# Projecting 63 of a graph's 64 nodes on the right side of a two-layer graph attention kernel

## The chip, the core and the metric

The kernel runs on one core of a Trainium2 chip. The metric is the device time of one execution in microseconds (us), the lower the better. The engines are TensorE (PE, with its weight loads listed apart as PEld), VectorE (DVE), ScalarE (ACT), GpSimd (POOL) and SyncE (SP), which issues most DMAs.

## What is computed

There are 128 graphs of 64 nodes with 768 features each. After a layer norm and a ReLU, two layers of the following run, and the input is added at the end:

```python
adj_tri = jnp.triu(adj, k=1)
diag_mask = jnp.triu(adj, k=0) - adj_tri
h = hidden_state
for l in range(L):
    m_left = jnp.einsum('bsh,oh->bso', h, W_left[l])
    m_right = jnp.einsum('bsh,oh->bso', h, W_right[l])
    u_left = jnp.einsum('bih,bjh->bij', h, m_left) / temper
    u_right = jnp.einsum('bih,bjh->bij', h, m_right) / temper
    u = u_left * adj_tri + u_left * diag_mask + u_right * jnp.swapaxes(adj_tri, 1, 2)
    delta_exp_u = jnp.exp(u) * adj
    attention = delta_exp_u / (jnp.sum(delta_exp_u, axis=2, keepdims=True) + 1e-10)
    h_lin = jnp.einsum('bsh,oh->bso', h, W_lin[l]) + b_lin[l]
    ctx = jnp.matmul(attention, h_lin)
    h = jax.nn.relu(_layer_norm(ctx, ln_a[l], ln_b[l]))
```

In the sum for `u` the right scores are multiplied by the transposed strict triangle: entry (i, j) counts only where i > j. For i = 0 there is no such j, so the right scores of row i = 0 are always multiplied by zero.

## The kernel before

**Tiles and groups.** A tile is 128 rows of `h`, that is two graphs. A group is four tiles (`TILES`), eight graphs. Each layer has 16 groups, so there are 32 groups in all. Every product is made in three passes over operands that are split into a high and a low part of type float32r (`PASSES`, line 47): high by high, low by high, high by low.

**The buffer of the split rows.** `ht` (line 190) holds the transposed rows of a group, with the features on the partitions. Within a tile, a part's 128 columns are ordered by node and then by graph: column 2n + b is node n of graph b (`ht_half`, line 278, and `by_graph`). So the first two columns of a tile are node 0 of both graphs.

**The projections (M steps).** `project` (line 541) does one job k of 12: the block `oc = k // 2` of 128 output features, and the side `k % 2` (0 left, 1 right). The left and right weights are taken untransposed, so the job projects each node i to the vector that is later multiplied by the rows of all j. A job has 6 feature blocks by 3 passes, that is 18 matmuls over all four tiles, with 512 columns each, into one of two banks of `pm` (`M_BANKS`). The jobs k = 0 and k = 1 are done in two halves of two tiles each (`m_parts`, line 57), so they take 36 matmuls of 256 columns each. A right-side matmul thus has 512 columns for k = 3, 5, 7, 9, 11 and 256 columns for k = 1.

**Emptying a job.** ACT writes the high part of the bank into `gt` (line 678), and DVE writes the low part (line 754, through the helper at line 722). Both read through `by_node`, which turns the order by node into an order by graph, and write through `gt_part`. TensorE may start job k when the job k - 2 has been emptied (`m_clear`, line 573).

**The scores (S steps).** Line 597 multiplies a tile's `ht` columns by 256 columns of `gt`: for one graph, its 64 columns of both parts and both sides. There are 8 such matmuls for each block `oc`, and 6 blocks in a group.

**After the scores.** U, EX, EM, EP and ET make the masked exponentials. H (line 609) makes the third projection in jobs of 18 matmuls with 384 columns each. C (line 633) multiplies both. T (line 537) transposes the rows of the next group with 128-column matmuls. F normalises. A (line 620) transposes adjacency tiles with 128-column matmuls in layer 0. `mask` has the triangles in it already: line 795 multiplies the scores by them.

**What sets the order.** The order of the steps is written out by hand in `iteration_steps` (line 99) and `m_phase_steps` (line 64), and every engine walks the same list. Each engine is its own queue and waits on semaphores. The middle groups are loops whose bodies are one group.

**Start.** POOL sets the constants (lines 483 to 506) and counts `const_ready` up to 10; PE, ACT and DVE wait for that before their first work. SP issues the first loads of rows, weights, adjacency and vectors without waiting for POOL (lines 405 to 411). The next load of rows (line 399, called at line 426) waits for the transposes of tile 0 (line 424).

The functions touched by the change are `gt_part` (line 286), `by_node` (line 290), the POOL block (line 482), the PE block (line 527) with `project`, and the places at lines 678 and 753 that call `by_node`.

Of the kernel before, what the change touches and what calls it, by code (L numbers as in the profile page):

```python
# [36 lines left out]
F32 = mybir.dt.float32  # L37
# [5 lines left out]
HI, LO = 0, 1  # L43
LEFT, RIGHT, LIN = 0, 1, 2
ML, ADJ, MR = 0, 1, 2

PASSES = ((HI, HI), (LO, HI), (HI, LO))

M_BANKS = 2
C_BANKS = 2  # L50
TILES = 4
# [101 lines left out]
def gnn_kernel(nc, x, adj, w_left, w_right, w_lin, b_lin, ln_a, ln_b, h1, adj_t, out):  # L153
    B, S, _ = adj.shape
    H = x.shape[2]
    L = w_left.shape[0]
    P = 128
# [23 lines left out]
    with ExitStack() as ctx:  # L181
# [3 lines left out]
        def sem(name):  # L185
            return ctx.enter_context(nc.semaphore(name))


        wt = sb("wt", [P, 3, 2, KC, H], F32R)
        ht = sb("ht", [P, KC, TILES, 2, P], F32R)  # L190
        gt = sb("gt", [P, 2, 2, 2, ROWS], F32R)
# [30 lines left out]

        const_base = sem("const_base")
        const_ready = sem("const_ready")
        vec_loaded = sem("vec_loaded")
        adj_loaded = sem("adj_loaded")
        adj_t_stored = sem("adj_t_stored")
# [5 lines left out]
        m_hi = sem("m_hi")  # L233
# [48 lines left out]
        def by_graph(tiles):  # L282

            return tiles.rearrange("p c (b n) -> p c b n", b=2)

        def gt_part(k, part):

            return gt[:, k // 2 % 2, part, k % 2, :].rearrange("p (t b n) -> p t b n", t=TILES, b=2)

        def by_node(bank):  # L290

            return bank.rearrange("p (t n b) -> p t b n", t=TILES, b=2)


# [186 lines left out]
        @block.gpsimd  # L481
        def _(pool):
            nc.gpsimd.memset(ident[:], 0.0).then_inc(const_base, 1)
            nc.gpsimd.memset(until[:], 1.0).then_inc(const_base, 1)
            nc.gpsimd.memset(beyond[:], 1.0).then_inc(const_base, 1)
            nc.gpsimd.memset(ebd[:], 0.0).then_inc(const_ready, 1)
            nc.gpsimd.memset(powers[:, 0:1], 0.5).then_inc(const_ready, 1)
            nc.gpsimd.memset(powers[:, 1:2], -0.5).then_inc(const_ready, 1)
            nc.gpsimd.memset(unit[:, HI, :], 1.0).then_inc(const_ready, 1)
            nc.gpsimd.memset(unit[:, LO, :], 0.0).then_inc(const_ready, 1)  # L490
            pool.wait_ge(const_base, 3)
            pool.wait_ge(const_ready, 5)

            nc.gpsimd.affine_select(out=ident[:], in_=ident[:], compare_op=ALU.not_equal, fill=1.0, base=0,
                                    pattern=[[1, P]], channel_multiplier=-1).then_inc(const_ready, 1)

            for b in range(2):

                own = slice(b * S, (b + 1) * S)
                pool.wait_ge(const_ready, 6 + 2 * b)  # L500
                nc.gpsimd.affine_select(out=until[own, :], in_=until[own, :], compare_op=ALU.is_ge, fill=0.0, base=0,
                                        pattern=[[-1, S]], channel_multiplier=1).then_inc(const_ready, 1)
                pool.wait_ge(const_ready, 7 + 2 * b)
                nc.gpsimd.affine_select(out=beyond[own, :], in_=beyond[own, :], compare_op=ALU.is_gt, fill=0.0, base=0,
                                        pattern=[[1, S]], channel_multiplier=-1).then_inc(const_ready, 1)
            pool.wait_ge(const_ready, 10)

            def walk(part, G):
                first, end, looped, steps, _, _ = part
                for step in steps:  # L510
                    kind = step[0]
                    if kind == "C":
                        t = step[1]
                        pool.wait_ge(c_var, tile_count(G, t + 1))
                        nc.gpsimd.tensor_tensor(col[:, STD, t:t + 1], col[:, VAR, t:t + 1], powers[:, 0:1],  # L515
                                                ALU.pow).then_inc(c_std, 1)
                    if kind == "X":
                        t = step[1]
                        pool.wait_ge(x_var, tile_count(G + step[2], t + 1))
                        nc.gpsimd.tensor_tensor(col[:, XRSTD, t:t + 1], col[:, XVAR, t:t + 1], powers[:, 1:2],  # L520
                                                ALU.pow).then_inc(x_rstd, 1)

            each_part(pool, walk)
# [2 lines left out]
        @block.tensor  # L526
        def _(pe):
            pe.wait_ge(const_ready, 10)

            def transposes(part, G, step, source):  # L530

# [9 lines left out]
            def project(k, t0, t1, c0, c1):  # L541

                oc, lr = k // 2, k % 2
                for kc in range(c0, c1):
                    for n, (a, b) in enumerate(PASSES):
                        last = nc.tensor.matmul(pm[:, k % M_BANKS, t0 * P:t1 * P], wt[:, lr, a, kc, oc * P:(oc + 1) * P],  # L546
                                                ht[:, kc, t0:t1, b, :], start=(kc == 0 and n == 0),
                                                stop=(kc == KC - 1 and n == len(PASSES) - 1))
                return last

# [93 lines left out]
        def _(act):  # L644
# [5 lines left out]
            def walk(part, G):  # L650
# [3 lines left out]
                for step in steps:  # L654
# [14 lines left out]
                    elif kind == "V":  # L669
                        _, slot, count = w_slot(first, step)  # L670
                        act.wait_ge(w_loaded[slot], count)
                        _, mat, ob = step
                        nc.scalar.copy(wt[:, mat, HI, :, ob * P:(ob + 1) * P],
                                       side[:, slot, :].rearrange("p (c n) -> p c n", c=KC)).then_inc(v_hi, 1)
                    elif kind == "M" and step[3] == TILES and step[5] == KC:
                        k = step[1]
                        act.wait_ge(m_full, M_JOBS * N + k + 1)
                        nc.scalar.copy(gt_part(k, HI), by_node(pm[:, k % M_BANKS, :])).then_inc(m_hi, 1)  # L678
                    elif kind == "H":
                        t, half = step[1:]  # L680
                        j = H_JOB + 2 * t + half
                        act.wait_ge(m_full, M_JOBS * G + j + 1)
                        nc.scalar.copy(hl[:, H_SLOTS[t], HI, SUMS + half * HALF:SUMS + (half + 1) * HALF],  # L683
                                       pm[:, j % M_BANKS, 0:HALF]).then_inc(m_hi, 1)
                    elif kind == "U":

                        p = step[1]
                        wait_from(act, stored[p], 32 * G)
                        act.wait_ge(u_full, tile_count(G, 2 * p + 2))
                        for b in range(2):  # L690
                            near, far = slice(b * S, (b + 1) * S), slice((1 - b) * S, (2 - b) * S)
                            nc.scalar.copy(parted[p][near].rearrange("p t a m j -> p t (a m j)"),
                                           pu[far, 2 * p:2 * p + 2, b * 2 * P:(b + 1) * 2 * P]).then_inc(u_cross, 1)
                    elif kind == "EX":
                        act.wait_ge(u_summed, pair_count(G, 2))
                        nc.scalar.activation(us[:], us[:], ACT.Exp, scale=INV_TEMPER).then_inc(e_exp, 1)
                    elif kind == "ET":
                        act.wait_ge(e_moved, 32 * G + 32)
                        nc.scalar.copy(et[:, :, HI, :], ebd[:]).then_inc(et_hi, 1)
                    elif kind == "N":  # L700
                        t = step[1]
                        act.wait_ge(x_shift, tile_count(G + step[2], t + 1))
                        row = rows[:, H_SLOTS[t], :]
                        nc.scalar.activation(row, row, ACT.Relu, bias=col[:, XSHIFT, t:t + 1],  # L704
                                             scale=col[:, XRSTD, t:t + 1]).then_inc(x_norm, 1)
                    elif kind == "F" and layer == 0:
                        t = step[1]
                        act.wait_ge(f_affine, tile_count(G, t + 1))
                        nc.scalar.activation(side[:, t % 2, :], side[:, t % 2, :], ACT.Relu).then_inc(f_done, 1)  # L709
# [5 lines left out]
        def _(dve):  # L715
# [5 lines left out]
            def low_part(dst, src, hi):  # L721
                return nc.vector.tensor_tensor(dst, src, hi.bitcast(F32), ALU.subtract)  # L722

            def walk(part, G):
# [3 lines left out]
                for step in steps:  # L728
# [21 lines left out]
                    elif kind == "M" and step[3] == TILES and step[5] == KC:  # L750
                        k = step[1]
                        dve.wait_ge(m_hi, M_JOBS * N + k + 1)
                        low_part(gt_part(k, LO), by_node(pm[:, k % M_BANKS, :]), gt_part(k, HI)).then_inc(m_clear, 1)
                    elif kind == "H":
                        t, half = step[1:]
                        j = H_JOB + 2 * t + half
# [154 lines left out]
```

## Time and profile before

| what | value |
|---|---|
| time, median of 3 runs | 2858.11 us |
| lowest and highest of the 3 | 2855.97 and 2859.23 us |
| the profiled execution, span from first to last instruction | 2857.3 us |
| instructions in the span | 43013 |
| PE busy | 2820.9 us (99%) |
| PEld busy | 2577.6 us (90%) |
| DVE busy | 1546.2 us (54%) |
| ACT busy | 691.1 us (24%) |
| POOL busy | 109.6 us (4%) |

For the profiled execution the trace gives the span alone, and it lies within the three times. Its matmuls overlap each other, so a matmul's mean duration is longer than the spacing from one to the next; the spacing is read from the chain of work that ended last, where a run of matmuls stands with its count and the time that it took.

### The profile page before, as it was taken

Reading aid. Unit: us, or ns where it says so; the run is one execution under the profiler, and the core shown is the slowest. Engines: PE = TensorE matmul, PEld = TensorE weight load, DVE = VectorE, ACT = ScalarE, POOL = GpSimd, SP = SyncE. Lnnn points to the kernel's source line nnn. Section 1 sums busy time; section 2 is a strip of 40 time slices with the busy share of each in tenths; the row PEclk is TensorE's granted clock in tenths of the full one; section 3 lists DMA queues with packets and bytes.
Section 4 is the critical chain, followed back from the end, with each engine's and each line's share of the span. In section 5 each row is a group of like instructions: output and inputs, shape, how many; then the busy total and the mean of one; then the engine's idle time right before and its main releaser. Section 6 shows DMA issues by size and latency. Waiting matters only on the chain.

```text
span 2857.3 us, 43013 instructions
## 1 busy us (share of the span) xinstructions
PE 2820.9 (99%) x15880; PEld 2577.6 (90%) x15880; DVE 1546.2 (54%) x3426; ACT 691.1 (24%) x1271; POOL 109.6 (4%) x209
## 2 busy tenths in 40 slices
PE   7999999999999999999999999999999999999997
PEld 6999899998899988999989999899998899998996
DVE  5555565555555555655555555455545555554556
ACT  3322222322223222232332222112221122221121
POOL 0000000000000000000000000000000000000000
PEclk9999999999999999999999999999999999999998
DMA  5111011110111111111241121121211111111211
GB/s 160 40 41 42 34 51 40 46 44 26 49 40 46 44 40 35 46 46 52 62 127 57 55 61 61 55 72 50 61 61 53 63 54 56 61 61 55 72 34 57
DMA packets 127178, 157.63 MB, mean 55 GB/s; under 512 B 65440, under 2 KB 83872, under 8 KB 127136
## 3 DMA queue, kind: packets, MB, share of 16 engines
q1 hardware_dynamic: 125984, 153.91, 17.6%
q10 hardware_dynamic: 1152, 3.15, 0.4%
q8 instruction: 28, 0.46, 0.1%
q14 instruction: 14, 0.11, 0.0%
HBM read 100.40 MB, written 52.43 MB: 53 GB/s over the span
## 4 chain that ended last, share of the span: by engine, by line
PE 98%; DVE 1%; DMA 1%; SPq 0%; ACT 0%; issue 0%; DVEq 0%; ACTq 0%
PE pm L546 55%; PE pm L609 28%; PE pu L597 6%; PE pc L633 5%; PE pc L537 3%; DMA rows<-in_x_dram 0%; DMA side<-in_L_gnn_W_lin_dram 0%; PE pu L620 0%; SPq L389 0%; SPq L378 0%; DVE side L789 0%; DVE rows L852 0%; DVE side L852 0%; DVE rows L842 0%; DVE side L842 0%
## 5 line engine op out<-in xcount | busy, mean ns | idle before, releaser
L546 PE MATMUL pm<-ht,wt 128*128 128x256 f32 (+1 forms) x8064 | 1636.5, 360 | 1.3 <-DVE ht L722 1.3
L546 PEld LDWEIGHTS pm<-ht,wt 128*128 128x128 f32 x8064 | 1352.7, 189 | 215.6 <-issue 1.7
L609 PE MATMUL pm<-wt,ht 128*128 128x384 f32 x4608 | 845.4, 337 | 0.6 <-DVE hl L722 0.6
L609 PEld LDWEIGHTS pm<-wt,ht 128*128 128x128 f32 x4608 | 794.0, 188 | 6.8 <-DVE hl L722 6.8
L722 DVE TENSOR_TENSOR gt<-pm,gt 128x512 fp32r<-128x512 f32 x384 | 265.4, 691 | 814.4 <-ACT gt L678 814.4
L678 ACT CAST gt<-pm 128x512 fp32r<-128x512 f32 x384 | 224.0, 583 | 1197.6 <-PE pm L546 1197.6
L722 DVE TENSOR_TENSOR hl<-pm,hl 128x384 fp32r<-128x384 f32 x256 | 142.5, 557 | 390.6 <-ACT hl L683 389.6
L683 ACT CAST hl<-pm 128x384 fp32r<-128x384 f32 x256 | 123.0, 480 | 551.1 <-PE pm L609 551.1
L597 PEld LDWEIGHTS pu<-gt,ht 128*128 128x128 f32 x1536 | 211.6, 196 | 9.7
L597 PE MATMUL pu<-gt,ht 128*128 128x256 f32 x1536 | 214.7, 282 | 0.0
L633 PE MATMUL pc<-hl,et 128*128 128x386 f32 (+1 forms) x768 | 158.7, 342 | 3.1 <-DVE et L722 1.8
L515 POOL TENSOR_TENSOR col<-col,powers 128x1 f32<-128x1 f32 x128 | 72.1, 563 | 2087.4 <-DVE col L836 2087.4
L633 PEld LDWEIGHTS pc<-hl,et 128*128 128x128 f32 x768 | 137.9, 190 | 9.1 <-DVE et L722 2.3
L822 DVE SCALAR_TENSOR_TENSOR side<-vec,col,pc 128x384 f32<-128x384 f32 x252 | 143.7, 612 | 4.5
L722 DVE TENSOR_TENSOR ht<-pc,ht 128x384 fp32r<-128x384 f32 x256 | 130.2, 550 | 2.8 <-ACT ht L661 2.6
L852 DVE SCALAR_TENSOR_TENSOR side<-side,col,vec 128x768 f32<-128x768 f32 x126 | 128.3, 1019 | 4.4
L828 DVE BATCH_NORM_STATS2 stats<-side 128x6 f32<-128x384 f32 x252 | 127.8, 550 | 0.0
L842 DVE SCALAR_TENSOR_TENSOR side<-side,mom,vec 128x768 f32<-128x768 f32 x126 | 127.3, 1010 | 0.5
L537 PE MATMUL pc<-ident,rows 128*128 128x128 f32 x768 | 106.4, 275 | 14.5 <-ACT rows L704 11.6
L661 ACT CAST ht<-pc 128x384 fp32r<-128x384 f32 x256 | 116.4, 516 | 5.2 <-PE pc L537 4.9
L709 ACT ACTIVATE side<-side 128x768 f32<-128x768 f32 x64 | 54.2, 846 | 253.4 <-DVE side L852 253.4
L537 PEld LDWEIGHTS pc<-ident,rows 128*128 128x128 f32 x768 | 92.2, 141 | 19.5 <-issue 10.7
(60 smaller groups left out, 848.5 us busy)
## 6 DMA issues: line engine op xcount, KB each, us to landing
rows<-in_x_dram SPq DMA_DIRECT2D x64, 384.0 KB, 3.2
h_dram<-side SPq DMA_DIRECT2D x64, 384.0 KB, 2.3
rows<-h_dram SPq DMA_DIRECT2D x64, 384.0 KB, 3.2
side<-in_x_dram SPq DMA_DIRECT2D x64, 384.0 KB, 3.3
out_dram<-side SPq DMA_DIRECT2D x62, 384.0 KB, 2.6
mask<-in_adj_dram SPq DMA_DIRECT2D x48, 128.0 KB, 3.6
side<-in_L_gnn_W_left_dram SPq DMA_DIRECT2D x12, 384.0 KB, 3.7
side<-in_L_gnn_W_right_dram SPq DMA_DIRECT2D x12, 384.0 KB, 3.6
```

The lines of the kernel that those rows point to most:

```text
L537: last = nc.tensor.transpose(pc[:, half, j * P:(j + 1) * P], source[:, kc * P:(kc + 1) * P], ident[:])
L546: last = nc.tensor.matmul(pm[:, k % M_BANKS, t0 * P:t1 * P], wt[:, lr, a, kc, oc * P:(oc + 1) * P], ht[:, kc, t0:t1, b, :], start=(kc == 0 ...
L597: last = nc.tensor.matmul(pu[:, t, b * 2 * P:(b + 1) * 2 * P], h_parts[:, b, :], gt[:, oc % 2, :, :, own], start=(oc == 0 and b == 0), sto ...
L609: last = nc.tensor.matmul(pm[:, j % M_BANKS, 0:HALF], ht[:, kc, t, a, :], wt[:, LIN, b, kc, half * HALF:(half + 1) * HALF], start=(n == 0) ...
L633: last = nc.tensor.matmul(pc[:, half, 0:own.stop - own.start], et[:, t, a, :], hl[:, H_SLOTS[t], b, own], start=(n == 0), stop=(n == 2))
L678: nc.scalar.copy(gt_part(k, HI), by_node(pm[:, k % M_BANKS, :])).then_inc(m_hi, 1)
L683: nc.scalar.copy(hl[:, H_SLOTS[t], HI, SUMS + half * HALF:SUMS + (half + 1) * HALF], pm[:, j % M_BANKS, 0:HALF]).then_inc(m_hi, 1)
L722: return nc.vector.tensor_tensor(dst, src, hi.bitcast(F32), ALU.subtract)
L822: nc.vector.scalar_tensor_tensor(out=context[:, at], in0=vec[:, 0, at], scalar=col[:, ESUM, t:t + 1], in1=pc[:, half, behind:behind + HALF ...
L828: nc.vector.bn_stats(stats[:, half, :], context[:, half * HALF:(half + 1) * HALF]).then_inc(c_stats, 1)
L842: nc.vector.scalar_tensor_tensor(out=row, in0=row, scalar=mom[:, t, 0:1], in1=vec[:, 1, :], op0=ALU.subtract, op1=ALU.mult).then_inc(f_cen ...
L852: nc.vector.scalar_tensor_tensor(out=row, in0=row, scalar=col[:, SCALE, t:t + 1], in1=vec[:, 2, :], op0=ALU.mult, op1=ALU.add).then_inc(f_ ...
```

## The change

The right side of a job has 126 columns for a tile in place of 128: the two columns of node 0 are left out. The bank then holds 4 x 126 columns (or 2 x 126 in a half job). ACT and DVE read the shorter bank and write nodes 1 to 63 into `gt`. The columns of node 0 of the right side in `gt` are set to zero once at the start, by four memsets on POOL, and stay so. PE has one more wait at its start, for these memsets.

```diff
+RIGHT_SIDE = 1
...
+        first_zero = sem("first_zero")
...
+        def nodes(k):
+
+            return S - k % 2
+
         def gt_part(k, part):
 
-            return gt[:, k // 2 % 2, part, k % 2, :].rearrange("p (t b n) -> p t b n", t=TILES, b=2)
-
-        def by_node(bank):
-
+            both = gt[:, k // 2 % 2, part, k % 2, :].rearrange("p (t b n) -> p t b n", t=TILES, b=2)
+            return both[:, :, :, k % 2:S]
+
+        def by_node(k):
+
+            bank = pm[:, k % M_BANKS, 0:TILES * 2 * nodes(k)]
             return bank.rearrange("p (t n b) -> p t b n", t=TILES, b=2)
...
             nc.gpsimd.memset(beyond[:], 1.0).then_inc(const_base, 1)
+            for half in range(2):
+                for part in (HI, LO):
+                    unused = gt[:, half, part, RIGHT_SIDE, :].rearrange("p (g n) -> p g n", n=S)[:, :, 0:1]
+                    nc.gpsimd.memset(unused.bitcast(F32), 0.0).then_inc(first_zero, 1)
             nc.gpsimd.memset(ebd[:], 0.0).then_inc(const_ready, 1)
...
             pe.wait_ge(const_ready, 10)
+            pe.wait_ge(first_zero, 4)
...
                 oc, lr = k // 2, k % 2
+                cols = 2 * nodes(k)
                 for kc in range(c0, c1):
                     for n, (a, b) in enumerate(PASSES):
-                        last = nc.tensor.matmul(pm[:, k % M_BANKS, t0 * P:t1 * P], wt[:, lr, a, kc, oc * P:(oc + 1) * P],
-                                                ht[:, kc, t0:t1, b, :], start=(kc == 0 and n == 0),
+                        last = nc.tensor.matmul(pm[:, k % M_BANKS, t0 * cols:t1 * cols], wt[:, lr, a, kc, oc * P:(oc + 1) * P],
+                                                ht[:, kc, t0:t1, b, P - cols:P], start=(kc == 0 and n == 0),
                                                 stop=(kc == KC - 1 and n == len(PASSES) - 1))
...
-                        nc.scalar.copy(gt_part(k, HI), by_node(pm[:, k % M_BANKS, :])).then_inc(m_hi, 1)
+                        nc.scalar.copy(gt_part(k, HI), by_node(k)).then_inc(m_hi, 1)
...
-                        low_part(gt_part(k, LO), by_node(pm[:, k % M_BANKS, :]), gt_part(k, HI)).then_inc(m_clear, 1)
+                        low_part(gt_part(k, LO), by_node(k), gt_part(k, HI)).then_inc(m_clear, 1)
```

## Rows read from the trace of the kernel before

**Rows 1.** The page: span, busy engines, TensorE's clock in 40 slices, the chain.

```profile
span 2857.3 us, 43013 instructions
...
PE 2820.9 (99%) x15880; PEld 2577.6 (90%) x15880; DVE 1546.2 (54%) x3426; ACT 691.1 (24%) x1271; POOL 109.6 (4%) x209
...
PEclk9999999999999999999999999999999999999998
...
PE 98%; DVE 1%; DMA 1%; SPq 0%; ACT 0%; issue 0%; DVEq 0%; ACTq 0%
```

**Rows 2.** Waits of PE: line, waited for: us in total, times, longest.

```profile
PE pc L537 <- ACT rows L704: 11.6, 2, 7.5
...
PE pc L633 <- DVE et L722: 1.8, 1, 1.8
PE pm L546 <- DVE ht L722: 1.3, 1, 1.3
```

**Rows 3.** Groups of PE's instructions, shapes apart: count | busy us, mean ns | idle before.

```profile
L546 PE MATMUL pm<-ht,wt 128*128 128x512 f32 x5760 | 1347.7, 391 | 0.0
L609 PE MATMUL pm<-wt,ht 128*128 128x384 f32 x4608 | 845.4, 337 | 0.6 <-DVE hl L722 0.6
L546 PE MATMUL pm<-ht,wt 128*128 128x256 f32 x2304 | 291.4, 285 | 1.3 <-DVE ht L722 1.3
L597 PE MATMUL pu<-gt,ht 128*128 128x256 f32 x1536 | 214.7, 282 | 0.0
...
L537 PE MATMUL pc<-ident,rows 128*128 128x128 f32 x768 | 106.4, 275 | 14.5 <-ACT rows L704 11.6 <-DVE ht L722 2.9
```

**Rows 4.** The chain in order of time, 1070 to 1130 us: start us, us, what, count.

```profile
1070.83 3.12 PE pm L609 x18
1073.95 0.66 PE pc L537 x6
...
1078.41 6.46 PE pm L546 x54
...
1088.08 0.44 PE pu L620 x4
...
1097.80 0.95 PE pu L597 x8
...
1107.89 4.10 PE pm L546 x18
...
1118.12 8.19 PE pm L546 x36
```

**Rows 5.** Groups of the instructions that write `gt`, on DVE and ACT.

```profile
L722 DVE TENSOR_TENSOR gt<-pm,gt 128x512 fp32r<-128x512 f32 x384 | 265.4, 691 | 814.4 <-ACT gt L678 814.4
...
L678 ACT CAST gt<-pm 128x512 fp32r<-128x512 f32 x384 | 224.0, 583 | 1197.6 <-PE pm L546 1197.6
```

**Rows 6.** Timeline, 0 to 20 us: start us, us, engine, line, operation [idle before, releaser].

```profile
1.12 0.52 POOL L486 MEMSET ebd<- 128x512 f32 x1
1.58 0.10 POOL L487 MEMSET powers<- 128x1 f32 x1
1.61 0.10 POOL L488 MEMSET powers<- 128x1 f32 x1
...
3.35 0.24 POOL L504 TENSOR_SCALAR_AFFINE_SELECT beyond<-beyond 64x64 bf16<-64x64 bf16 x1
...
3.94 1.02 DVE L865 BATCH_NORM_STATS2 xstats<-rows 128x6 f32<-128x384 f32 x2 [2.96 <-DMA rows<-in_x_dram]
...
7.46 1.51 PE L537 MATMUL pc<-ident,rows 128*128 128x128 f32 x6 [7.46 <-ACT rows L704]
```

**Rows 7.** The chain in order of time, 0 to 45 us, at the fourth load of rows.

```profile
11.16 0.43 SPq L389
11.60 0.04 issue
11.64 9.06 DMA rows<-in_x_dram
```

## The prediction, made before the changed kernel ran

> **What bounds the kernel now.** I read the page first. PE is busy for 99% of the span, the chain of work that ended last is 98% PE, and TensorE's clock is granted in full, 2.4 GHz, in nearly every slice [rows 1]. So the time is the time of the matmuls, and an edit is worth what it takes out of PE's stream. Then I read what PE waits for: its longest wait is 7.5 us and belongs to the start; the projections at L546 waited once, for 1.3 us [rows 2]. No other engine holds PE up once the groups run. Third come the groups of PE's instructions with the shapes kept apart: the 512-column and the 256-column matmuls of L546 are the ones that the change cuts [rows 3]. Their mean durations overlap, so they are no prices. The price is the spacing, which I read from the chain in order of time: a run of one kind with its count and its time [rows 4].
>
> **The price of a column.** All from [rows 4]. Eighteen matmuls of 512 columns took 4.10 us, 227.8 ns each. Fifty-four of 256 columns took 6.46 us, 119.6 ns each. The slope is (227.8 - 119.6) / 256 = 0.423 ns a column, and what is left at no columns is 119.6 - 256 x 0.423 = 11.4 ns. The line is tested by a third width: at 384 columns it gives 173.7 ns, and eighteen such matmuls took 3.12 us, 173.3 ns each. So between 256 and 512 columns a matmul of these operands costs 11.4 ns and 0.423 ns for each column, and nothing else shows. One more reading matters for the new operand, which is 126 columns of each tile in turn: L597 reads its 256 columns in four pieces of 64, and eight of them took 0.95 us, 118.8 ns each, no more than L546's two pieces of 128. Pieces cost nothing by that.
>
> The Trainium skill has a rule that speaks against this price: the page "TensorE: Matmul & The Clock Gate", section "Back-to-back issue gap", gives a sustained spacing of about 81 ns at 128 columns and 131 ns at 512 for a stream of weight loads and matmuls. That slope is 0.13 ns a column, and by it the sum below would be, as an estimate, 3.6 us in place of 11.7. The trace does not agree: at 512 columns it shows 227.8 ns, not 131 [rows 4], so I give the rule no chance of its own.
>
> **The change, part by part.**
>
> *The right-side jobs k = 3, 5, 7, 9, 11.* Of the 5760 matmuls of 512 columns [rows 3], five jobs in ten are right ones: 2880. Each goes to 504 columns, inside the tested widths: 8 x 0.423 = 3.38 ns. In all 2880 x 3.38 = 9.7 us. It all lies on the path, since PE is the path.
>
> *The right-side job k = 1.* Of the 2304 matmuls of 256 columns [rows 3], half are right ones: 1152. They go to 252 columns, which is narrower than any matmul of split operands in the trace. On the line this saves 4 x 0.423 = 1.69 ns each, 1.9 us in all. The trace has no such width, so I bound it. The lower bound is the line. The nearest narrower rows are the 128-column transposes: four took 0.44 us and six took 0.66 us, 110 ns each [rows 4], where the line would give 65.5. They are above the line, at 0.859 ns a column. At that rate 252 columns would take 216.5 ns, 96.9 ns more than now, and 1152 of them 111.6 us. The two ends are 1.9 us saved and 111.6 us lost. I take the line: 252 is 4 columns from a point on it and 124 from the transposes, which are another operation, on plain float32 operands.
>
> *The emptying by ACT and DVE.* Half of the 384 jobs write 504 elements in place of 512, in runs of 63. ACT takes 583 ns and DVE 691 ns for a job now, and both idle ahead of it, ACT for 1197.6 us in all and DVE for 814.4 [rows 5]. A job of 512 columns lasts 4.10 us on PE, and a bank is wanted again only when the other bank's job has ended. The two together take 1.27 us of that; even if the shorter runs doubled both, 2.55 us would fit. I cost it at nothing either way. The cover would be gone only if they took over 4.10 us together.
>
> *The four memsets on POOL.* They stand in POOL's queue ahead of the rest of the constants, so that `const_ready` comes later. Small memsets take 0.10 us each, started 0.03 apart; the largest took 0.52 [rows 6]. So four cost between 0.1 and 2.1 us of POOL's time, nearer to the small ones at 8 elements a partition: up to 0.4 us. POOL ends its constants at 3.59 us, and DVE's first work starts at 3.94, when the first rows land [rows 6]. With 0.4 us more it starts some 0.05 us later. That does not reach the end either: PE's first transposes end at 8.97 us [rows 6], while the load that waits for them is issued at 11.64, straight behind SP's own earlier issues, and this load is what the chain follows up to 20.70 us [rows 7]. There are 2.6 us to spare, more than the upper bound of 2.1. I cost the memsets at nothing.
>
> *The wait of PE for the memsets.* It stands in front of PE's whole queue, but PE's first transposes wait for ACT until 7.46 us [rows 6], long after POOL is through. Nothing.
>
> *What is unchanged.* The number of matmuls, weight loads, DMAs and other waits stays; PE's scores at L597 still read 256 columns, the zeros among them.
>
> *What is late next.* PE comes 0.36 us sooner through each of the 32 groups (11.7 / 32). DVE at 54% and ACT at 24% [rows 1] have to follow in 0.36 us less for each group and have the room, so no new wait is due.
>
> **The sum.** 9.7 + 1.9 = 11.7 us with the rounding left to the end (9.74 + 1.95). Against the profiled span that is 2857.3 - 11.7 = 2845.6 us. The trace gives no other time for that execution; its span lies 0.8 us under the median of the three runs, 2858.1, and within their spread. I predict the median: 2858.1 - 11.7 = 2846.4 us, 0.4% less. About 0.2% (5.7 us) is what a measurement of this kernel can tell from no change, so the forecast is faster by twice that.
>
> **The rivals.**
>
> *The narrow matmuls leave the line (slower).* One mechanism, at the two halves of job k = 1: TensorE takes matmuls that are narrower than 256 columns at another rate. For it: no matmul of split operands under 256 columns is in the trace, and the only narrower ones, the transposes, cost 110 ns where the line gives 65.5 [rows 4]. Against it: these transposes differ in operation and type, so their rate may belong to that and not to the width; and the line shows no bend down to 256. The price at their rate is 111.6 us less the 9.7 of the wide jobs: 2858.1 + 111.6 - 9.7 = 2960 us. It decides from 8.5 ns extra for a narrow matmul (9.74 us / 1152), where it eats the whole gain. I give it 0.20.
>
> The Trainium skill, page "FP8 and Floating Point Precision", section "TensorE Precision Notes", says that true float32 takes four passes through the array and that a reduced-precision float32 exists beside it; it does not say when the one turns into the other. If the narrow matmuls fell to four passes, the estimate would be 1008 columns on the line, 437.5 ns, and 3214 us in all; no run so far shows it.
>
> *Width buys nothing (no change).* The moving operand is fetched in whole aligned pieces, so that 126 columns which start 8 bytes into a tile cost as much as 128 from its start, at both widths. For it: the widths that price the line, 256, 384 and 512, are all multiples of 128, and these matmuls start at a tile's first column. Against it: the line through the three is smooth [rows 4], though such a grain would not show in it. The time is then 2858 us. That the slices in the diff did not shorten the matmuls at all would give the same; the shapes in the diff speak against that. Together 0.16.
>
> The Trainium skill names such pieces: the page "SBUF — State Buffer", in the section on the DMA port swizzle, speaks of 16-byte lines and a penalty for each line crossed. By it 126 columns from byte 8 touch 32 lines, as many as 128 columns do, which is this rival's no gain; no run here shows the lines.
>
> **How the numbers follow.** The forecast, faster along the line, has 0.64; no change 0.16; slower 0.20. The likeliest case's own range is 2844 to 2850 us: at the low end the full 11.7 us from a run near the lowest of the three (2855.97), at the high end only the wide jobs gain (2858.1 - 9.7 = 2848.4) with the spread of the three runs above it. The range that holds 8 in 10 reaches to the no-change case with its spread, 2843.5 to 2859.5, and leaves the slower rival out. The cases give faster 0.64, within 0.2% 0.16, slower 0.20.
>
> **What would show each step right or wrong.** In the profile after, the groups by shape should show 2880 matmuls of L546 with 504 columns and 1152 with 252. In the chain, eighteen of 504 columns should take 4.04 us (224.4 ns each) where eighteen of 512 still take 4.10, and eighteen of 252 should take 2.12 us (117.9 ns) beside 2.15 for 256. A run of eighteen narrow ones at 3.9 us would be the slower rival; 4.10 us at 504 columns would be the no-change one. The waits of PE should stay the handful at the start; a new one on `m_clear`, from DVE at L722, would prove the emptying mis-costed, and a later end of the fourth load of rows than 20.70 us would prove the memsets mis-costed.

## The result and the profile after

The changed kernel takes 2874.14 us (median of 5 runs, 2873.72 to 2874.35) against 2856.57 us before in the same comparison: a ratio of 1.006, 95% interval 1.0049 to 1.007. It is slower by 17.6 us, where 11.7 us less were predicted.

The page after shows the same picture as [rows 1], with the added time on TensorE alone:

```profile
span 2872.5 us, 43018 instructions
...
PE 2835.7 (99%) x15880; PEld 2575.7 (90%) x15880; DVE 1543.7 (54%) x3426; ACT 690.0 (24%) x1271; POOL 109.7 (4%) x213
...
PEclk9999999999999999999999999999999999999998
...
PE 98%; DVE 1%; DMA 1%; SPq 1%; ACT 0%; issue 0%; DVEq 0%; ACTq 0%
```

The clock did not change and PE is still the bound. (A time lies some 1.8 us above its span: this profiled execution took 2874.26 us. So the profiled execution before, with a span of 2857.3 us, was one of the slowest of its kernel, and the spans differ by 15.2 us only.) The waits of PE after answer to [rows 2]:

```profile
PE pc L550 <- ACT rows L718: 10.5, 2, 7.5
PE pc L550 <- DVE ht L736: 4.0, 1, 4.0
...
PE pm L560 <- DVE ht L736: 1.6, 2, 1.3
```

No new wait holds PE up. The groups after, which answer to [rows 3], show the new shapes:

```profile
L560 PE MATMUL pm<-ht,wt 128*128 128x504 f32 x2880 | 700.0, 396 | 0.0
L560 PE MATMUL pm<-ht,wt 128*128 128x512 f32 x2880 | 685.5, 391 | 0.0
...
L560 PE MATMUL pm<-ht,wt 128*128 128x256 f32 x1152 | 152.6, 287 | 1.6 <-DVE ht L736 1.6
L560 PE MATMUL pm<-ht,wt 128*128 128x252 f32 x1152 | 147.2, 281 | 0.0
```

The change does what it says: 2880 matmuls have 504 columns and 1152 have 252. But a matmul of 504 columns lasts 396 ns, longer than one of 512 with 391. The narrow ones seem to get shorter. The chain of the changed kernel in order of time (start, us, what, count) gives the spacing, as in [rows 4]:

```profile
1084.37 6.46 PE pm L560 x54
...
1091.89 2.11 PE pm L560 x18
...
1094.43 8.34 PE pm L560 x36
...
1104.79 8.32 PE pm L560 x36
...
1114.07 4.09 PE pm L560 x18
...
1119.23 4.14 PE pm L560 x18
...
1124.33 8.33 PE pm L560 x36
...
1133.62 8.32 PE pm L560 x36
```

The chain of the kernel before has the same pieces, beside those of [rows 4]:

```profile
1085.93 2.15 PE pm L546 x18
...
1088.51 8.21 PE pm L546 x36
...
1098.76 8.18 PE pm L546 x36
...
1113.06 4.11 PE pm L546 x18
```

The piece of 18 ahead of the first 36 is the second half of k = 1 at 252 columns: 2.11 us, where the kernel before took 2.15. The first half lies within the piece of 54, which takes 6.46 us as before [rows 4]: there the four columns were worth nothing. A piece of 36 is a left job and a right job in turn (k = 2 and 3, then 4 and 5): 8.34 and 8.32 us against 8.21 and 8.18. The left job k = 6 alone still takes 4.09 us, so a right job takes about 4.23 us, 235 ns a matmul in place of 227.8, where 4.04 us were due.

For a finer reading, I take the start times of the trace's records and the gaps from one matmul of a job to the next: the mean of the sixth to the seventeenth gap, over all groups, without gaps above 300 ns, in which another step stands between. A spacing below is this mean. Left jobs: 226.7 to 227.7 ns before and 226.7 to 226.9 after. Right jobs k = 3, 5, 9, 11: 226.7 ns before, 234.5 after; k = 7, which follows other work: 230.1. Summed over the four pieces of the chain the right jobs lose 0.57 us a group (0.13 to 0.14 us each, and 0.03 for k = 7, whose eighteen take 4.14 us, against 4.11 in the chain before), times 32 groups 18 us, less 1.3 us (0.04 x 32) for the second half of the narrow job: about 17 us, which is the loss.

### The profile page after: what moved, and what is told of

Its sections match the earlier page's. It is cut to its first block, busy times and chain, and to the rows that moved or that the text cites. A ratio compares the mean times of both kernels' runs of the same rounds, so it can differ in the third digit from the quotient of the medians.

```text
span 2872.5 us, 43018 instructions
## 1 busy us (share of the span) xinstructions
PE 2835.7 (99%) x15880; PEld 2575.7 (90%) x15880; DVE 1543.7 (54%) x3426; ACT 690.0 (24%) x1271; POOL 109.7 (4%) x213
## 3 DMA queue, kind: packets, MB, share of 16 engines
q1 hardware_dynamic: 125984, 153.91, 17.6%
q10 hardware_dynamic: 1152, 3.15, 0.4%
## 4 chain that ended last, share of the span: by engine, by line
PE 98%; DVE 1%; DMA 1%; SPq 1%; ACT 0%; issue 0%; DVEq 0%; ACTq 0%
PE pm L560 55%; PE pm L623 28%; PE pu L611 6%; PE pc L647 5%; PE pc L550 3%; DMA rows<-in_x_dram 0%; DMA side<-in_L_gnn_W_lin_dram 0%; PE pu L634 0%; SPq L397 0%; SPq L386 0%; DVE side L803 0%; SPq L407 0%; DVE rows L866 0%; DVE side L866 0%; DVE rows L856 0%
## 5 line engine op out<-in xcount | busy, mean ns | idle before, releaser
L560 PE MATMUL pm<-ht,wt 128*128 128x256 f32 (+3 forms) x8064 | 1651.5, 362 | 1.6 <-DVE ht L736 1.6
L736 DVE TENSOR_TENSOR gt<-pm,gt 128x512 fp32r<-128x512 f32 (+1 forms) x384 | 263.4, 686 | 830.3 <-ACT gt L692 830.3
L692 ACT CAST gt<-pm 128x512 fp32r<-128x512 f32 (+1 forms) x384 | 222.8, 580 | 1212.8 <-PE pm L560 1212.8
```

The source lines that it names most:

```text
L560: last = nc.tensor.matmul(pm[:, k % M_BANKS, t0 * cols:t1 * cols], wt[:, lr, a, kc, oc * P:(oc + 1) * P], ht[:, kc, t0:t1, b, P - cols:P], ...
L692: nc.scalar.copy(gt_part(k, HI), by_node(k)).then_inc(m_hi, 1)
```

## The experiments

**The wide jobs alone.** k = 1 goes back to 256 columns:

```diff
-            return S - k % 2
+            return S - (1 if k % 2 and k > 1 else 0)
...
-            return both[:, :, :, k % 2:S]
+            return both[:, :, :, S - nodes(k):S]
```

> Only the right-side jobs k = 3, 5, 7, 9, 11 are narrowed to 504 columns; k = 1 keeps its 256 columns. In the changed kernel the 504-column matmuls follow each other at about 234 ns, not the 224 of the line, where the 512-column ones still take 228. All theories agree here: if the loss is in the wide jobs alone (6 ns x 2880 = 17 us), this kernel takes about 2874 to 2875 us, since k = 1 gains about 1 us at 252 columns. If the narrow job had a part in the loss, it would take under 2870 us.

2875.97 us, ratio to before 1.0074 (1.0057 to 1.0091). The loss is the wide jobs'.

**The narrow job alone.** Only k = 1 is cut (`1 if k == 1 else 0`).

> The change at the job k = 1 alone: 1152 matmuls of 252 columns, and all wide jobs at 512. By the prediction's line it gains 1.9 us; by the chain of the changed kernel (eighteen in 2.11 us against 2.15) about 1.3 us; by the slower rival of the prediction it loses. About 2855 us, not to be told from no change.

2855.14 us, ratio 0.9995 (0.9985 to 1.0004): no change that can be measured, as expected. The matmuls of 252 columns take some 120 ns in the first half of k = 1 and 117 in the second, against 120 at 256 columns in the kernel before and 117.9 on the line. The slower rival of the prediction is out.

**Start, run or width.** Three kernels change the moving operand of the wide right-side jobs. The first takes the first 126 columns of a tile:

```diff
...
-                                                ht[:, kc, t0:t1, b, P - cols:P], start=(kc == 0 and n == 0),
+                                                ht[:, kc, t0:t1, b, 0:cols], start=(kc == 0 and n == 0),
```

> As the kernel with the wide jobs alone, but the 126 columns of a tile are its first ones (nodes 0 to 62), so that the moving operand starts where the tile starts; the right scores of node 63 are left out of those blocks. Theory A, the start 8 bytes into a tile is what costs: the spacing falls to the line's 224.4 ns and the time to 2858 - 9.7 = about 2847 us. Theory B, runs of 126 columns with jumps between them are what costs, and theory C, the width of 504 itself breaks the rhythm of weight loads and matmuls: the spacing stays at 234 ns and the time at 2874 us.

The second keeps 512 columns and moves the start (`first` is 2 for the high part and 126 for the low part, in the tile's 256 columns of both):

```diff
...
+                return ht[:, kc, t0:t1].rearrange("p t a n -> p t (a n)")[:, :, first:first + P]
...
```

> The kernel before with its 512 columns and runs of 128, but in the right-side jobs from k = 3 on each run starts off the tile's start, 8 bytes past a 16-byte boundary, so it reads two columns of the neighbouring part (the right scores of those blocks are of other data). Theory A (the start): the spacing rises from 228 to about 238 ns, the time to about 2858 + 28 = 2886 us. Theories B (runs of 126) and C (the width of 504): the spacing stays at 228 ns and the time at 2858 us.

The third reads 504 columns in one unbroken run:

```diff
...
+                return ht[:, kc].rearrange("p t a n -> p (t a n)")[:, b * 512:b * 512 + 504]
...
```

> As the kernel with the wide jobs alone, but the 504 columns are one unbroken run that starts at the buffer's first column of the feature block (for the low part, at column 512), so the right scores of those blocks are of other data. Theory A (the start) and theory B (the short runs with jumps): the spacing falls to 224.4 ns and the time to about 2847 us. Theory C (the width of 504 as such): the spacing stays at 234 ns and the time at 2874 us.

| kernel | time, us | ratio to before | spacing in right jobs, ns |
|---|---|---|---|
| 504 from the first column | 2856.32 | 1.0002 (0.9992 to 1.0012) | 226.7 |
| 512, shifted start | 2901.20 | 1.0162 (1.0145 to 1.0179) | 242.2 |
| 504 in one run | 2857.06 | 1.0003 (0.9993 to 1.0012) | 226.7 |

The chain of the kernel with 504 from the first column shows a pair of jobs (k = 4 and 5) in the time of before:

```profile
1098.94 8.19 PE pm L560 x36
```

The chain of the kernel with the shifted start shows the same pair:

```profile
1112.89 8.46 PE pm L553 x36
```

No theory had it all. The start costs: 15.5 ns at full width, and the whole loss goes when the 504 columns start with the tile. Runs do not count here: one run or four give 226.7 ns. But from an aligned start 504 columns cost exactly what 512 cost, so the line of the prediction fails there too.

**A ladder of widths.** Each of the five right jobs gets another width, from an aligned start, once as one run and once as four:

```diff
-            return S - (1 if k % 2 and k > 1 else 0)
+            return {3: 62, 5: 61, 7: 60, 9: 59, 11: 56}.get(k, S)
...
```

The single runs are read as in the kernel with one run, the four as in the one with the first columns.

> The five wide right-side jobs read one unbroken run from an aligned start, each of another width: 496, 488, 480, 472 and 448 columns for k = 3, 5, 7, 9, 11 (the right scores of those blocks are of other data and partly left out). Theory D, TensorE's time goes in blocks of 16 columns (504 costs what 512 costs): 220.0, 220.0, 213.3, 213.3 and 200.0 ns, 38 us less than before in all, about 2818 us. Theory E, blocks of 32 columns: 226.7, 226.7, 213.3, 213.3 and 200.0 ns, about 2825 us. The line of the prediction: 220.9, 217.5, 214.2, 210.8 and 200.6 ns, about 2814 us.

> As the run before it, with the same five widths, but as four runs of a quarter each that start at the tiles' first columns (124, 122, 120, 118 and 112 columns a run; the last nodes' right scores are left out). If only the width of the whole matmul is rounded up, the five spacings are those of the single runs. If each run is rounded up by itself, to 16 columns, they are 226.7, 226.7, 226.7, 226.7 and 200.0 ns; to 4 columns (16 bytes), 220, 223, 213, 213 and 200 before the whole is rounded.

| columns | the prediction's line, ns | one run, ns | four runs, ns |
|---|---|---|---|
| 504 | 224.6 | 226.7 | 226.7 |
| 496 | 221.2 | 220.0 | 225.0 |
| 488 | 217.8 | 224.2 | 224.5 |
| 480 | 214.4 | 216.7 | 216.7 |
| 472 | 211.1 | 213.6 | 213.4 |
| 448 | 200.9 | 202.7 | 204.8 |

One run each: 2825.14 and 2829.26 us, against 2859.93 for the kernel before beside them. Neither blocks of 16 nor of 32 columns fit: 488 takes longer than 496, in one unbroken run. And runs do count at some widths: at 496 columns four cost 5 ns more than one. The line is off by 1 to 7 ns at these widths, and what a cut of 8 columns is worth on it, 3.4 ns, lies within that error.

**A ladder of starts.** All jobs at 512 columns, the starts of the right ones 2, 4, 8, 16 and 32 columns off:

```diff
...
+                off = {3: 2, 5: 4, 7: 8, 9: 16, 11: 32}[k]
+                first = P - off if b == LO else off
...
```

> The full 512 columns in four runs of 128 in all jobs, but in the right-side jobs k = 3, 5, 7, 9, 11 each run starts 2, 4, 8, 16 and 32 columns (8, 16, 32, 64 and 128 bytes) off the tile's start (the right scores of those blocks are of other data). An eighteen at a shift of 2 took 4.36 us before (242 ns), against 4.10 (227.8). If the grain of the start is 16 bytes, only the job k = 3 is slow and the time is about 2865 us; 32 bytes: k = 3 and 5, about 2874 us; 64 bytes: k = 3, 5 and 7, about 2883 us; if any start off the tile's is slow, all five, about 2901 us.

Spacing 242.2, 229.0, 233.1, 230.9 and 233.3 ns; 2878.32 us in one run of the kernel. The chain of that kernel has the five in order (k = 2 and 3; 4 and 5; 6; 7; 8 and 9; 10 and 11):

```profile
1097.34 8.49 PE pm L568 x36
...
1107.87 8.23 PE pm L568 x36
...
1117.05 4.10 PE pm L568 x18
...
1122.22 4.19 PE pm L568 x18
...
1127.37 8.28 PE pm L568 x36
...
1136.61 8.30 PE pm L568 x36
```

The start of 8 bytes is the worst, but even 128 bytes (k = 11) cost 6.6 ns. So no grain of up to 128 bytes in the start alone explains it.

**Starts and cuts together.** Five operands in one kernel:

```diff
...
+                whole = ht[:, kc].rearrange("p t a n -> p (t a n)")
+                if k == 3:
+                    return whole[:, b * 512 + 2:b * 512 + 2 + 4 * cols]
+                off = {5: 4, 7: 8, 9: 2, 11: 16}[k]
+                return ht[:, kc, t0:t1, b, off:off + cols]
...
```

> Starts and cuts together, in the right-side jobs: k = 3 one unbroken run of 504 columns from column 2; k = 5 four runs of 124 from column 4; k = 7 four of 120 from column 8; k = 9 four of 124 from column 2 (ending short of the tile's end); k = 11 four of 112 from column 16. If the start costs something for each run, k = 3 is near 228 to 229 ns (a quarter of the 7 ns that four runs cost at 504); if it costs by the matmul, 234 ns. If only starts off a 16-byte boundary cost, k = 5, 7 and 11 have the spacing of their widths from an aligned start, and k = 9 lies some 7 ns above its own.

Spacing 230.0 ns (504 in one run from column 2), 226.2 (four of 124 from column 4), 220.0 (four of 120 from column 8), 233.3 (four of 124 from column 2) and 204.8 (four of 112 from column 16); 2844.93 us in one run of the kernel. At 124 columns a run, column 2 costs 8.3 ns over the aligned 225.0, and column 4 costs 1.2; column 8 costs 3.3 at 120 columns, and column 16 nothing at 112. One run from column 2 costs 3.3 ns, four cost 7.8: more than a quarter, so the price is neither by the run nor by the matmul alone.

**The rows' buffer or the weights moved.** In the changed kernel, `ht` goes 56 bytes on, or `wt` 8 bytes on:

```diff
-        ht = sb("ht", [P, KC, TILES, 2, P], F32R)
+        ht = sb("ht", [P, KC * TILES * 2 * P + 16], F32R)[:, 14:14 + KC * TILES * 2 * P].rearrange(
+            "p (c t a n) -> p c t a n", c=KC, t=TILES, a=2)
```

The move of the weights is written in the same way, with `2:` in place of `14:`. It makes `wt` 64 bytes longer, so the buffers behind it, `ht` first, lie 64 bytes further on.

> The changed kernel with the buffer of the split rows put 56 bytes further on, so that column 2 of a tile lies on a 64-byte boundary and column 0 lies 8 bytes ahead of one. Theory A1, the start matters by its own address: the right-side jobs of 504 columns fall from about 234 to 226.7 ns (as from the first column), and the left-side jobs of 512, which now start off the boundary, rise from 226.7 to about 242; in all about 2857 + 45 = 2902 us. Theory A2, what matters is where the moving operand lies against the weights that are read at the same time: the same, since the weights have not moved. Theory A3, the start within the tile matters and not the address: nothing changes, 2874 us.

> The changed kernel with the weights put 8 bytes further on, the split rows on a 64-byte boundary as before, so that the 504 columns from column 2 lie against the weights as 512 columns from column 0 did. Theory A1 (the moving operand's own address): nothing changes in these jobs, about 234 ns and 226.7 ns, 2874 us (the third projection, which reads the weights as its moving operand, may change). Theory A2 (the address against the weights): the right-side jobs fall to 226.7 ns and the left-side ones rise above it.

With the rows moved, right jobs take 230.0 ns and left jobs 241.1 (2911.54 us); with the weights moved, right jobs take 230.0 and left jobs 230.7 (2881.10 us). The chain with the rows moved, at k = 2 and 3:

```profile
1107.10 8.49 PE pm L561 x36
```

The chain with the weights moved, at k = 4 and 5:

```profile
1106.13 8.29 PE pm L561 x36
```

The second kernel is not the one that its expectation describes, since the rows move too: by 64 bytes, with the weights 8 bytes on. In both kernels the rows so lie 56 bytes further from the weights than before. The right jobs take 230.0 ns in both, but the left ones take 241.1 and 230.7: the distance between the two (theory A2) does not settle the price alone. Theory A1 had the left jobs right with the rows moved (about 242 ns), but it foresaw 226.7 ns for the right ones, and nothing new with the weights moved, as the rows lie on a 64-byte boundary there too; it falls as well, and so does A3. That the place of the weights counts cannot be read from this pair; the kernels with shifted weights below show it.

**Both moved by 8 bytes,** in the kernel before, with the two edits above and `2:` in both:

> The kernel before, with 512 columns everywhere, but both the weights and the split rows put 8 bytes further on. The two have the same place against each other as before. If only that place counts, the 512-column matmuls stay at 226.7 ns and the time at 2857 us. If the start of the moving operand counts by its own address, they rise to about 241 ns (as when the split rows alone were off) and the time to about 2857 + 5760 x 14.5 ns + the narrow ones = 2941 us or more.

2961.99 us, 242.2 to 244.4 ns in all wide jobs. The chain has a pair of jobs (k = 2 and 3) at 8.74 us, against 8.21 before:

```profile
1126.53 8.74 PE pm L548 x36
```

Here too the longer `wt` pushes `ht` on, so that the rows move by 72 bytes and the weights by 8, and they lie 64 bytes further apart than the expectation has it. The kernels with shifted weights below have that distance without a start off the boundary, where the weights are read 16 columns ahead: 512 columns take 229.0 ns there. So the distance is not everything: at the same distance, both operands 72 bytes further on, 8 bytes off their 64-byte boundary, cost 13 to 15 ns more.

**One weight for all.** The right jobs load the same weight columns eighteen times:

```diff
...
+                if lr == 1 and k > 1:
+                    a, kc = HI, 0
+                return wt[:, lr, a, kc, oc * P:(oc + 1) * P]
...
```

> The changed kernel, but the right-side jobs from k = 3 on load the same 128 weight columns for all 18 matmuls (wrong right scores), so that the weights' addresses stop changing from matmul to matmul. If the loss comes from the moving operand alone, the spacing stays at 234 ns and the time at 2874 us. If it comes from weight reads that collide with the moving reads by address, the spacing changes, by more than 2 ns in either direction.

2874.73 us and 234.5 ns in k = 3, 5, 9, 11, 230.1 in k = 7, the same to 0.1 ns. This did not settle what it was meant to: the blocks that a job reads lie whole multiples of 1024 bytes apart, so a place that counts within a shorter stretch was left as it was.

**The weights shifted.** The weights are read some columns ahead of their place, under 504 columns from the first column and from column 2:

```diff
...
+                at = oc * P + {1: -2, 2: -4, 3: -8, 4: -16, 5: -64}.get(oc, 0)
+                return wt[:, lr, a, kc, at:at + P]
...
```

The second kernel has the shifts -2, -4, -16, -32 and -64 in the same place. No buffer moves in either.

> The 504 columns from the tile's first column (226.7 ns, as the 512 ones), with the weights read 2, 4, 8, 16 and 64 columns ahead of their place for the jobs k = 2 and 3, 4 and 5, 6 and 7, 8 and 9, 10 and 11 (all scores wrong from there on). If rounding of the width alone keeps 504 from gaining, all five stay at 226.7 ns. If the weight reads get in the way of the moving reads, the spacing at 504 changes with the shift and for some shift falls towards the line's 223 to 224 ns, and the 512-column jobs change too (with the weights 8 bytes off they took 230.7).

> The 504 columns from column 2 (234.5 ns) with the weights read 2, 4, 16, 32 and 64 columns ahead for the five pairs of jobs. If the start of the moving operand alone costs, all five right-side jobs stay at 234 ns. If it is the moving reads against the weight reads, they differ by the shift, 230 ns or less at some; a shift with less than 226 ns at 504 and 226.7 at 512 would allow a kernel that beats both.

| weights ahead by, columns | 504 from column 0, ns | 512 beside it, ns | 504 from column 2, ns | 512 beside it, ns |
|---|---|---|---|---|
| 2 | 233.3 | 233.3 | 231.0 | 233.3 |
| 4 | 226.7 | 226.8 | 231.3 | 228.4 |
| 8 | 226.7 | 233.3 | - | - |
| 16 | 230.0 | 229.0 | 226.7 | 229.0 |
| 32 | - | - | 233.3 | 232.6 |
| 64 | 226.7 | 226.8 | 234.5 | 226.7 |

(2866.67 and 2878.45 us, one run each.) The chain of the first shows its pair at a shift of 2 columns (k = 2 and 3), in 8.38 us against 8.21 before:

```profile
1090.88 8.38 PE pm L566 x36
```

With nothing changed but the address of the weights, the same matmuls go from 226.7 to 233.3 ns and back. No shift brought 504 columns under 226.7. And for the slow start at column 2, a shift of 16 columns gave 226.7 (in k = 7, which the change alone had at 230.1), while for the start at column 0 the same shift cost 3.3 ns. So neither place has a price of its own: with the weights in place column 0 is the fast start, with the weights 16 columns ahead it is column 2.

**The loss taken back.** So the last kernel is the changed kernel whole, with the right side's weights moved on by 448 bytes, and the third projection's weights and all buffers behind them by 512. Counted within blocks of 512 bytes, the right side's weights alone move, 64 bytes nearer to the start:

```diff
-        wt = sb("wt", [P, 3, 2, KC, H], F32R)
+        whole = sb("wt", [P, 3 * 2 * KC * H + P], F32R)
...
+                first = mat * 2 * KC * H + (0, P - 16, P)[mat]
...
```

> The changed kernel with nothing left out, and the right side's weights alone put 16 columns (64 bytes) nearer to the start of a 512-byte block than the others; left side and third projection keep their places. With the weights read 16 columns ahead, one job of 504 columns from column 2 took 226.7 ns. If the loss of the change is where the two reads lie against each other, all right-side jobs fall from 234.5 to about 226.7 ns and the time to about 2874 - 2880 x 7.5 ns = 2853 to 2857 us, level with the kernel before. If the start at column 2 costs by itself, or that one job was a lucky phase, they stay at 230 to 234 ns and the time at 2863 to 2874 us.

2856.94 us, ratio to the kernel before 1.0002 (0.9992 to 1.0011). Its groups show the 504-column matmuls at 390 ns in place of 396:

```profile
L569 PE MATMUL pm<-ht,wt 128*128 128x504 f32 x2880 | 682.5, 390 | 0.0
```

Its chain shows a pair of jobs at 8.19 us, as before the change:

```profile
1098.26 8.19 PE pm L569 x36
```

The spacing is 226.7 to 226.8 ns in all five right jobs. The whole loss is gone, with the same columns from the same start, as expected. The rows moved by 512 bytes as well, which was not tested apart; but the left jobs, whose weights stayed, kept 226.7 to 227.8 ns, and in the changed kernel the jobs k = 3, 5, 9 and 11 took 234.5 ns alike, with weights that start whole multiples of 512 bytes apart.

## Why the prediction was wrong

**Right.** PE bounds the kernel before and after. The memsets cost nothing that the runs show: the four took 0.22 us of POOL and ended the constants at 3.73 us in place of 3.59, and DVE started at 3.84 us, as the rows landed.

The timeline of the changed kernel, from its start, has it:

```profile
1.12 0.22 POOL L497 MEMSET gt<- 128x8 f32 x4
...
3.49 0.24 POOL L516 TENSOR_SCALAR_AFFINE_SELECT beyond<-beyond 64x64 bf16<-64x64 bf16 x1
...
3.84 1.02 DVE L879 BATCH_NORM_STATS2 xstats<-rows 128x6 f32<-128x384 f32 x2 [2.86 <-DMA rows<-in_x_dram]
```

One of the prediction's own signs did come up. The fourth load of rows was issued at 12.72 us in place of 11.64 [rows 7], and landed at 21.17, later than 20.70:

```profile
12.72 8.45 DMA rows<-in_x_dram
```

Without the memsets it was issued at 10.56 and 11.48 in two experiments, and with them at 11.11 to 11.74 in three more and at 12.20 in a fourth. The two overlap, so this is taken for SP's own spread; at 0.5 us it would be a small part of the 17.6 in any case. Emptying stayed hidden: ACT took 577 ns and DVE 682 for the cut jobs, a little less than [rows 5], and runs of 63 cost nothing. That pieces cost nothing held for 504 columns from the tile's start, where one run and four took the same; it did not hold from column 2 (230.0 ns in one run, 234.5 in four) or at 496 columns (220.0 and 225.0). The term of k = 1 had the right sign: 1.3 us by the chain instead of 1.9, all of it in the second half.

**The step that failed** is the first term, "Each goes to 504 columns, inside the tested widths: 8 x 0.423 = 3.38 ns". It was to gain 9.7 us and lost about 18. It failed twice. First, the three widths of the line, 256, 384 and 512, do not test what lies between them, and the one in the middle is of L609, where the weights are streamed and the rows loaded: from an aligned start 504 columns take 226.7 ns, not 224.6 or less, and around them the widths scatter by several ns. That took the gain. Second, the term priced the columns and not the address: it left out that the operand now starts 8 bytes into a tile, against weights that stay where they were. That added 7.8 ns to a matmul (3.4 in k = 7). The prediction did name the new start, in the no-change rival, but bounded it at no gain; it gave no rival in which the start costs more than the columns save. An operand that no row showed was bounded from one side only.

**The rivals.** The slower one had the right sign for a wrong cause: it put the loss on the narrow matmuls, which lost nothing. The no-change one had half of the cause, a fetch that does not get cheaper by eight columns. Its mechanism of whole pieces is not borne out: 488 columns took longer than 496, and the changed kernel's 504 longer than 512. By the rule of 16-byte lines from the Trainium skill, page "SBUF — State Buffer", section on the DMA port swizzle, the cut operand would, as an estimate, cost what the full one costs; the trace shows 234.5 ns against 226.7, so the rule does not give this loss.

**The cause, as far as it is shown.** The loss depends on where the moving operand and the weights lie. It goes when the moving operand starts with the tile (2856.32 us), and it goes when the right side's weights move by 64 bytes within their 512-byte block (2856.94 us). The two places act together: which start is the fast one changes with the place of the weights. The weight loads themselves did not get longer, 2575.7 us of PEld in all after the change and 2577.6 before. In the records of the changed kernel the load of the next weights begins some 4 ns after a matmul has begun and lasts 188 ns, so both reads run at once. That they get in each other's way is the reading that fits; it is not shown what in the memory collides, nor by which grain. It was not found either why 504 columns never took less than 226.7 ns, in any placement tried (ten in the two kernels with shifted weights, seven more in the others); in these the eight columns are worth nothing.

## What to carry to other kernels

A price per column that is read from a few round, aligned widths does not hold to a few ns for a cut of 1 or 2 per cent: time the exact width at the exact start, or bound it by several ns a matmul to either side. Where TensorE is the bound and every matmul loads its own weights, the addresses of the two operands are a tuning knob of their own: here the same work took 226.7 or 234.5 ns a matmul, and moving one side's weights by 64 bytes within a 512-byte block decided it. A buffer that is made longer moves those behind it: work out where every operand lies before a move is called a test of one of them. Before a slice is cut from the front of a tile, ask whether it can be cut from the end: here that start took the loss away (2856.32 us), though it brought no gain.

## What was not expected of the hardware

The price of a matmul depends on the addresses of its two operands together. Matmuls of 512 columns with the same rows in the same place went from 226.7 to 233.3 ns when their weights were read 2 or 8 columns ahead of their place, and stayed at 226.8 at 4 columns ahead (228.4 in the second kernel). With both operands off their 64-byte boundary by 8 bytes, they took 242 to 244 ns and the kernel 2961.99 us, 3.7% more than the 2855.74 us beside it.

The Trainium skill, page "TensorE: Matmul & The Clock Gate", section "Step-by-step: what each phase is for", says that TensorE reads the streaming operand and the weights through two independent ports, and that loading the next weights does not steal read bandwidth from the running matmul. These traces do not agree that the two are without effect on each other: reading the weights 2 columns ahead, with nothing else moved, added 6.6 ns to each matmul of 512 columns (233.3 against 226.7).

The rhythm can also lock in two ways. In the changed kernel the right jobs that directly follow a left one (k = 3, 5, 9, 11) took 234.5 ns, and k = 7, which six matmuls of another step part from its left job, took 230.1, with gaps of 235 and 224 ns in turn. In the trace's first group k = 7 follows its left job directly, with both operands in the same place, and its first gaps are those of the others: 235, 238, 228, 234 and 237 ns. That points to what ran before, and not to the place; one group of 32 shows it.
